# Last stage's attention of a fused decoder layer: the exponentials become the matmul's weights, values with a column of ones move, and the stage's written-out order is replaced

## The reference, cut to what matters

```python
nx = _rmsnorm(X, g1)                       # X: 8 x 512 x 256
Q = (nx @ Wq.T).reshape(B, S, 4, 64).transpose(0, 2, 1, 3)
Kc = nx @ Wkc.T                            # one K and one V of width 64 for all 4 heads
Vc = nx @ Wvc.T
attn = softmax(einsum('bhsd,btd->bhst', Q, Kc) / 8, axis=-1)
out = einsum('bhst,btd->bhsd', attn, Vc)
X = X + out.transpose(0, 2, 1, 3).reshape(B, S, d) @ Wo.T
# then: norm, router (top 2 of 8 experts), shared expert, experts
```

## Time and profile before

| | |
|---|---|
| median of 3 executions | 1976.12 us (1971.84 to 1981.54) |
| profiled execution | 1981.15 us, span 1979.4 us |
| granted TensorE clock, mean | 0.959 |
| TensorE / VectorE / ScalarE / GpSimd busy over the span | 90% / 71% / 60% / 55% |
| `moe_attention` | about 1342 to 1750 us of the span |
| one turn in it | 45.4 us (mean of five: 1438.3 to 1665.5 us) |

### The profile page before, as it was taken

How to read it: one execution, slowest core, us unless ns; L and a number is a source line. 1 busy time by engine, 2 the same in 40 slices (tenths; PEclk the granted TensorE clock), 3 DMA queues, 4 the chain that set the end, 5 groups by cost and what they waited for, 6 DMA issues and landing times. The chain is left out here.

```text
span 1979.4 us, 46476 instructions
## 1 busy us (share of the span) xinstructions
PE 1779.3 (90%) x16808; PEld 986.1 (50%) x16808; DVE 1415.2 (71%) x3433; ACT 1185.8 (60%) x2285; POOL 1096.3 (55%) x1102
## 2 busy tenths in 40 slices
PE   5899999999999999889999999986998999779994
PEld 2566767676766767633233333222333344346662
DVE  5766676667676766477777888766699987757677
ACT  2666566566666666367677787782566666435552
POOL 2766666666676666543243433123667776646664
PEclk9999999999999999989899999897999999889998
DMA  6422222223222232321333212301001110224465
GB/s 197 103 66 66 66 66 66 66 66 76 66 66 66 60 82 66 71 65 34 54 65 65 50 37 46 60 11 38 22 23 44 49 49 33 73 73 130 116 209 201
DMA packets 102545, 141.36 MB, mean 71 GB/s; under 512 B 16400, under 2 KB 66352, under 8 KB 102320
## 3 DMA queue, kind: packets, MB, share of 16 engines
q1 hardware_dynamic: 95408, 119.44, 25.6%
q0 software_dynamic: 6912, 18.95, 2.7%
HBM read 53.77 MB, written 33.90 MB: 44 GB/s over the span
## 5 line engine op out<-in xcount | busy, mean ns | idle before, releaser
L821 POOL TENSOR_TENSOR a_P_lo<-a_PR,a_P_hi 128x384 f16<-128x384 f32 (+1 forms) x384 | 378.9, 1001 | 269.7 <-ACT a_PR L630 126.8
L1387 DVE TENSOR_REDUCE x_NM<-x_pm 128x1 f32<-128x512 f32 x512 | 342.5, 688 | 104.0 <-PE x_pm L1123 101.6
L1308 ACT ACTIVATE x_PR<-x_pS 128x512 f32<-128x512 f32 x512 | 300.8, 601 | 118.4 <-PE x_pS L1139 112.5
L739 DVE CUSTOM_DVE_ANT_0 a_pm<-a_pm,a_causal 128x128 f32<-128x128 f32 (+3 forms) x512 | 243.4, 511 | 133.2 <-PE a_pm L511 129.6
L630 ACT ACTIVATE a_PR<-a_pS 128x384 f32<-128x384 f32 (+1 forms) x384 | 202.4, 527 | 148.5 <-PE a_pS L535 145.6
L633 ACT ACTIVATE a_P_hi<-a_pS 128x384 f16<-128x384 f32 (+1 forms) x384 | 203.6, 530 | 26.6 <-PE a_pa L554 26.6
L1151 PE MATMUL x_pa<-x_PR,x_V 128*32 128x256 f32 x2048 | 170.9, 408 | 1.6
L511 PE MATMUL a_pm<-a_KA,a_QA 128*128 128x128 f16 (+3 forms) x512 | 125.3, 305 | 39.4 <-issue 21.6
L533 PE MATMUL a_pS<-a_QA,a_KA 128*128 128x512 f16 (+3 forms) x512 | 153.6, 303 | 1.2 <-ACT a_P_hi L633 0.8
L1462 POOL TENSOR_TENSOR x_res<-x_res,x_OT 128x256 f32<-128x256 f32 x32 | 23.5, 734 | 232.0 <-DVE x_OT L1396 232.0
L534 PE MATMUL a_pS<-a_QB,a_KB 128*128 128x512 f16 (+3 forms) x512 | 148.9, 304 | 0.0
(11 more groups left out here) (410 smaller groups left out, 5065.6 us busy)
## 6 DMA issues: line engine op xcount, KB each, us to landing
a_QA<-a_nat_q_hi SPq DMA_DIRECT2D x128, 128.0 KB, 2.3
first_keys<-sent SPq DMA_DIRECT2D x80, 129.0 KB
a_KA<-a_nat_k_hi SPq DMA_DIRECT2D x64, 128.0 KB, 2.3
a_KA<-a_nat_k_lo SPq DMA_DIRECT2D x64, 128.0 KB, 2.4
a_QB<-a_nat_q_lo SPq DMA_DIRECT2D x64, 128.0 KB, 2.3
a_KB<-a_nat_k_hi SPq DMA_DIRECT2D x64, 128.0 KB, 2.3
e_ga<-back SPq DMA_DIRECT2D x16, 512.0 KB
first_keys<-in_w SPq DMA_DIRECT2D x12, 512.0 KB
```

The source lines that it names most:

```text
L739: eng.tensor_tensor_reduce(out=pm[i % 2][:, 0:n], in0=pm[i % 2][:, 0:n], in1=causal[:, T - n:T], scale=1.0, scalar=NEG, op0=ALU.add, op1=A ...
L821: eng.tensor_tensor(P16[1][:, m % RH, 0:n], PR[:, m % RF, 0:n], P16[0][:, m % RH, 0:n], ALU.subtract).then_inc(s_el, 1)
L1308: eng.activation(PR[:, kc, j, :], pS[i % 2][:, :], ACT.Exp, scale=SCALE).then_inc(s_e, 1)
L1387: eng.tensor_reduce(NM[:, v % 2, c:c + 1], ring_bank("max", v, n)[:, :], AX.X, ALU.max, negate=True).then_inc(s_red, 1)
```

## The change

V gets a 65th column of ones, so that the sum of the exponentials comes out of the same matmul as the weighted values. In `weighted_values` the roles are exchanged: a block of 128 keys x 128 queries of PR is the weight matrix and the 65 columns of V move; the result has queries on partitions, 4 blocks of 65 columns in a bank, side 0 in pv and side 1 in pu. VectorE then takes 4 reciprocals (128 x 4) and 4 multiplications (128 x 256) per sequence, directly from the banks. Since the result is not transposed any more, Y is split in hi and lo (Y16, by ScalarE and GpSimd), TensorE transposes both (YT, 2 x 8 transposes) into pv and pu, and ScalarE copies these out (2 x 1024 float16 columns). Gone: the four additions on GpSimd, the four PU steps, Ln and Exp of the reciprocal, the copy PC. The table of positions is replaced as a whole by LAST_PLACE, for all engines.

```diff
-    V = sb("V", [P, 2, TT, D], F32)
-    ones32 = sb("ones32", [P, D], F32)
+    V = sb("V", [P, 2, TT, D + 1], F32)
 ...
             eng.wait_ge(s_e, 16 * b + 2 * i + 2)
             if i == 0:
                 eng.wait_ge(s_vo, b + 1)
-                after(eng, s_x1, 2 * b - 1)
+                after(eng, s_x1, 2 * b)
             elif i == TT:
-                eng.wait_ge(s_pc, b + 1)
+                eng.wait_ge(s_y, 4 * b + 2)
             for side in range(2):
-                m = eng.matmul(pv[half(side), :], V[:, par, kc, :], PR[:, i % 4, side, :], start=(kc == 0), stop=(kc == TT - 1))
+                for t in range(TT):
+                    m = eng.matmul(value_bank(side)[:, t * OW:t * OW + D + 1], PR[:, i % 4, side, t * P:(t + 1) * P], V[:, par, kc, :],
+                                   start=(kc == 0 and t == 0), stop=(kc == TT - 1), skip_group_check=True)
             m.then_inc(s_av, 1)

-        def exp_sums(b, j):
-            eng.wait_ge(s_ad, 4 * b + j + 1)
...
-            for side in range(2):
-                m = eng.matmul(pu[half(side), :], ones32[:, :], PR[:, 2 * j % 4, side, :], start=(j % 2 == 0), stop=(j % 2 == 1))
-            m.then_inc(s_pu, 1)
+        def turn_values(b, z):
+            eng.wait_ge((s_yh, s_yl)[z], 2 * b + 2)
+            if z == 0:
+                eng.wait_ge(s_y, 4 * b + 4)
+            for pair in range(2):
+                for t in range(TT):
+                    o = pair * T + t * P
+                    m = eng.transpose(value_bank(z)[:, :].bitcast(F16)[:, o:o + P], Y16[z][:, t, pair, :], k.id16[:, :])
+            m.then_inc(s_yt, 1)
...
                 for side in range(2):
                     eng.wait_ge(s_s, 16 * b + 2 * i + side + 1)
-                    after(eng, s_pu, 4 * b + i // 2 - 1)
+                    after(eng, s_av, 8 * b + i - 3)
                     eng.activation(PR[:, i % 4, side, :], pS[side][:, :], ACT.Exp, scale=SCALE).then_inc(s_e, 1)
...
-                eng.activation(RS[:, :], pu[:, :], ACT.Ln).then_inc(s_ln, 1)
-                eng.wait_ge(s_ln, 2 * b + pair + 1)
-                eng.activation(RS[:, :], RS[:, :], ACT.Exp, scale=-1.0).then_inc(s_rc, 1)
...
+                eng.activation(YT[z][:, :, :].rearrange("p a t -> p (a t)"), value_bank(z)[:, :].bitcast(F16), ACT.Copy).then_inc(s_yo, 1)
...
+                eng.reciprocal(RC[:, i, :], o[:, :, D]).then_inc(s_rc, 1)
+                eng.wait_ge(s_rc, 4 * b + i + 1)
+                eng.tensor_tensor(Y[:, :, pair, side, :], o[:, :, 0:D], RC[:, i, :].unsqueeze(2).to_broadcast([P, TT, D]),
+                                  ALU.mult).then_inc(s_y, 1)
...
-                eng.tensor_tensor(both, both, PR[:, (2 * j + 1) % 4, :, :], ALU.add).then_inc(s_ad, 1)
...
+LAST_PLACE = {
...
+    ("PE", "QK"): (7.224, 7.224, 8.938),
+    ("PE", "V"): (10.868,),
+    ("PE", "MX"): (1.193, 12.227, 16.689, 16.689, 28.543, 38.17, 41.193, 44.517),
+    ("PE", "NM"): (47.989,),
+    ("PE", "S"): (50.126, 55.366, 60.956, 71.226, 78.982, 83.035, 84.579, 89.259),
+    ("PE", "AV"): (81.063, 82.196, 82.196, 83.139, 87.157, 87.157, 91.495, 95.421),
+    ("PE", "YT"): (96.968, 96.968),
+    ("PE", "WO"): (100.505, 103.017),
...
+    ("PE", "O"): (153.929, 166.983),
+    ("PE", "RK"): (168.09,),
...
+    ("DVE", "QK"): (9.055, 9.055, 26.038),
+    ("DVE", "MX"): (26.038, 34.297, 34.297, 34.297, 34.297, 44.068, 44.068, 44.068),
+    ("DVE", "O"): (173.183, 173.183),
+    ("DVE", "R1"): (149.546,),
+    ("DVE", "R2"): (155.441,),
...
```

More of the change, by code:

```diff
@@ L1895, in moe_block @@
         moe_experts(nc, keep, inner, k, x_res, out_dram, B, groups, shared)
+LAST_TURN = 46.0
+LAST_PLACE = {
+    ("PE", "XT"): (3.925, 3.925),
+    ("PE", "QK"): (7.224, 7.224, 8.938),
[6 more added lines that the diff above has]
+    ("PE", "WO"): (100.505, 103.017),
+    ("PE", "FT"): (129.781, 129.781),
+    ("PE", "RT"): (140.121,),
+    ("PE", "H1"): (140.121, 142.004),
+    ("PE", "H3"): (142.004, 144.691),
+    ("PE", "O"): (153.929, 166.983),
+    ("PE", "RK"): (168.09,),
+    ("ACT", "N4"): (-8.58,),
+    ("ACT", "QK"): (3.454, 3.454, 10.717),
+    ("ACT", "V"): (10.717,),
+    ("ACT", "NM"): (37.914,),
+    ("ACT", "S"): (50.382, 60.419, 60.419, 66.48, 82.489, 82.489, 82.489, 82.489),
+    ("ACT", "YT"): (93.194, 93.194),
+    ("ACT", "YS"): (87.017, 88.012),
+    ("ACT", "F1"): (109.87,),
+    ("ACT", "F3"): (124.532,),
+    ("ACT", "H1"): (133.787, 133.787),
+    ("ACT", "H3"): (149.031, 149.031),
+    ("ACT", "R1"): (135.636,),
+    ("ACT", "R3"): (164.025,),
+    ("ACT", "SPLIT"): (44.585, 48.725),
+    ("DVE", "N1"): (-40.185,),
+    ("DVE", "N4"): (3.18,),
+    ("DVE", "XT"): (4.955, 4.955),
+    ("DVE", "QK"): (9.055, 9.055, 26.038),
+    ("DVE", "MX"): (26.038, 34.297, 34.297, 34.297, 34.297, 44.068, 44.068, 44.068),
+    ("DVE", "NORM"): (86.986, 86.986, 95.768, 95.768),
+    ("DVE", "WO"): (121.77, 121.77),
+    ("DVE", "F3"): (130.533,),
+    ("DVE", "FT"): (134.203, 134.203),
+    ("DVE", "RT"): (141.504,),
+    ("DVE", "H1"): (141.504, 143.365),
+    ("DVE", "H3"): (143.365, 146.171),
+    ("DVE", "O"): (173.183, 173.183),
+    ("DVE", "R1"): (149.546,),
+    ("DVE", "R2"): (155.441,),
+    ("DVE", "R3"): (176.043,),
+    ("DVE", "RK"): (172.773,),
+    ("DVE", "SPLIT"): (86.6, 86.6),
+    ("POOL", "NP1"): (7.955,),
+    ("POOL", "NP2"): (7.955,),
+    ("POOL", "YS"): (121.764, 121.764),
+    ("POOL", "NP3"): (144.717,),
+    ("POOL", "XR"): (144.717,),
+    ("POOL", "H3"): (171.595, 171.595),
+    ("POOL", "SC"): (207.713, 207.713, 207.713, 207.713),
+    ("SP", "MR"): (66.11,),
+}
@@ L2026, in at @@
         if step == "TB":
-            return b * TURN + PLACE["DVE", "RK"][0] + 0.1 + GAP * i
+            return b * LAST_TURN + LAST_PLACE["DVE", "RK"][0] + 0.1 + GAP * i
         if step in ("TL", "LD"):
-            return (groups[1].first - 1) * TURN + PLACE["DVE", "RK"][0] + GAP * Tables.STEPS + (0.01 if step == "TL" else 1.0)
-        return b * TURN + PLACE[engine, step][i]
+            return (groups[1].first - 1) * LAST_TURN + LAST_PLACE["DVE", "RK"][0] + GAP * Tables.STEPS + (0.01 if step == "TL" else 1.0)
+        return b * LAST_TURN + LAST_PLACE[engine, step][i]
     def at_split(engine, n):
@@ L2146, in sums @@
         def sums(b):
-            for j in range(4):
-                yield at("PE", "PU", b, j)
-                exp_sums(b, j)
+            for z in range(2):
+                yield at("PE", "YT", b, z)
+                turn_values(b, z)
             for h in range(2):
                 yield at("PE", "WO", b, h)
-                eng.wait_ge(s_y, 2 * b + 2)
-                eng.wait_ge(s_yl, 2 * b + 2)
+                eng.wait_ge(s_yo, 2 * b + 2)
                 for tt in range(2):
@@ L2310, in splits @@
                 weights.high(eng, n)
-        side_by_side(over(back), over(route), over(sums), over(values), over(exponentials), over(front), over(norm, 1), splits())
+        side_by_side(over(back), over(route), over(sums), over(exponentials), over(front), over(norm, 1), splits())
     def vector_program(eng):
@@ L2342, in sums @@
         def sums(b):
[L2343 to L2352, removed]
+            for i in range(H):
+                pair, side = i // 2, i % 2
+                yield at("DVE", "NORM", b, i)
+                o = value_bank(side)[:, 0:TT * OW].rearrange("p (t e) -> p t e", e=OW)
+                eng.wait_ge(s_av, 8 * b + TT * (pair + 1))
+                after(eng, s_yl, 2 * (b - 1) + pair + 1)
+                eng.reciprocal(RC[:, i, :], o[:, :, D]).then_inc(s_rc, 1)
+                eng.wait_ge(s_rc, 4 * b + i + 1)
+                eng.tensor_tensor(Y[:, :, pair, side, :], o[:, :, 0:D], RC[:, i, :].unsqueeze(2).to_broadcast([P, TT, D]),
+                                  ALU.mult).then_inc(s_y, 1)
             for h in range(2):
@@ L2583, in gpsimd_program @@
         eng.sem_inc(s_pre, 1)
-        side_by_side(over(back), over(route), over(sums), over(adds), over(norm, 1))
+        side_by_side(over(back), over(route), over(sums), over(norm, 1))
     def sync_program(eng):
```

66 lines of the change are left out of this document (21 added, 45 removed), and 6 rows, old and new, of the table PLACE.

## The result

The changed kernel takes 2028.1 us in the median (2021.7 to 2030.7, four executions) against 1975.9 us (1971.8 to 1981.5) in the same measurement: a ratio of 1.026, interval 1.022 to 1.029. The forecast was slower, by 1.3%, 2002 us; it became slower by 2.6%, twice as much, and within the range. The profiled execution took 2029.5 us, its span 2027.7.

The account below looks back on a forecast made before the run. TensorE's issue was taken as the bound, with about 3 us per turn lost behind VectorE. Terms +20 - 16 + 27 - 5 = +26 us gave 2002 us against the median of 1976.1, 1.3% slower; range 1955 to 2032.

Parts of the forecast that it names:

- The price of a value matmul: TensorE's AV steps: 128 records per sequence at 0.107 us each, set by the weight load; 14.0 us in all.
- the changes of shape: TensorE switching between full array and halves: 0.1 us each, 19 left of 34 per turn, 1.5 us less.
- Quick load: Rival, AV: weights load at the transposes' rate, 0.056 us a record, AV 7.5 us, total 1956 us; chance 0.16.
- load and stream one after the other: Rival, AV: load and stream don't overlap, 0.162 us a record, 56 us more, 2058 us; chance 0.06.
- YT: New transposes of Y on TensorE: 0.9 us per sequence, their inputs' delay covered by some 5 us of other work.
- The removed wait: TensorE's wait at XT for the low half of the normalized rows goes: -16 us.
- The added waits: TensorE waits at MX, RK and behind QK in the new order: 3.8 us per turn, seven times, +27 us.
- The other engines: VectorE even, GpSimd rid of four 2.45 us additions, ScalarE lighter; priced only through TensorE's waits.
- A turn of 48 to 49 us: Sign in the profile after: each turn of the stage takes 48 to 49 us, against 45.4 before.
- the last rival, the clock: More standing still lowers TensorE's clock more often; a stretch costs at most half its length; no chance given.

Follow-up runs that it names:

- mx_halves: Changed kernel with MX3 and MX4 moved apart, R1 and R2 later, and each value block as two 64-column halves; 1975.5 us, ratio 1.005.
- sc_later: Changed kernel with GpSimd's scatter issued later, behind its low rows of Y; 2017.9 us, ratio 1.027.
- cols33: Changed kernel with only 33 of the 65 value columns moving in each value matmul; 2064.3 us, ratio 1.051.
- col_halves: Changed kernel with each block of 128 weights as two of 64, side by side in TensorE's column halves; 1973.7 us, ratio 1.003.
- mx_only: Changed kernel with MX3 behind S3, MX4 behind O1 and VectorE's O0 ahead of MX3's reductions; 1981.0 us, ratio 1.006.
- sc_later_again: The changed kernel with the later scatter, same program run once more, on chip 3 instead of 13; 2031.6 us, ratio 1.028.
- old_order: Changed attention in the order of steps of the kernel before, with YT, NORM and YS placed in by hand; 2027.8 us, ratio 1.029.

## Why the prediction was right, and where its size was off

The direction and the price on which it hung came as forecast. The size did not: +52 us between the medians where the forecast had +26, and inside the range only because its upper side was kept wide. The two profiled executions are 48.3 us apart, of which 42.2 lie in the seven turns, 7.7 behind the last NM and -1.6 ahead of the first.

- **The price of a value matmul** (all hung on it): forecast 0.107 us a record, set by the load and not by the stream. Found: four matmuls, eight records, every 0.89 us, 0.112 each; with half the columns the same. A load record is 192 ns long by itself, as the slope of the earlier trace rows gives it (136 and 54), so at 0.112 apart each overlaps the next. Right, 0.005 low: AV 14.7 us a turn against 14.0. AV and YT together cost 3.9 us more than AV and PU did, where the forecast had 2.5 with the changes of shape. Quick load and "load and stream one after the other" are both out; 65 columns of streaming are hidden wholly.
- **YT** at 0.9 us, and covered: 0.90, with 0.6 us of waiting in all turns. Right, as long as GpSimd's scatter ends before; `mx_halves` shows the price without this cover, 6 us a turn.
- **The removed wait**, -16 us: XT and FT fell from 4.91 to 1.88 where no signal is held, 3.0 a turn. The wait itself is gone in the changed kernel as well, but there "issue" gaps fill its place (5.19).
- **The added waits**, 3.8 a turn: too high. Where no signal is held, MX rose by 1.0 (forecast 2.3), RK and O by 0.5 (0.7), QK and V by 0.2 (0.8), S by 1.0 (none): 2.7.
- **The other engines** got lighter as worked out (multiplications of 0.42 us); TensorE stayed the fullest, and no run shows what the relief was worth.
- **A turn of 48 to 49 us**: 48.4 in the profile of `sc_later`, 52.7 in that of the changed kernel. The span of `sc_later` is 26.7 us above that of before, forecast +26, but that is luck: +20.7 in the turns, +12 in the end, which holds the price of the later scatter, and -6 ahead of the first turn. And against before on its own chip its median is 48.5 us higher.
- **The step that was off in size** is the last rival, the clock, which I let only "widen the upper side", with no term for TensorE standing still while all is ready. In the changed kernel's profile this fills four of the seven turns (against `sc_later` H +2.3 and XT +3.3 a turn, S -0.7), with 6.8 us a turn at half clock, where `sc_later` has none. No term stood for the end either (+7.7). The trace of before showed held signals as well, up to 4.1 us late; I had not looked.

An estimate of the changed kernel where no signal is held: the start and the turns of `sc_later` (1362.3 and 318.2 us) and the end of `cols33` (314.9), both of chip 13, give 1997 us with the 1.75 around the span, and 2005 to 2010 with the 8 to 13 us by which the other executions of `sc_later` exceed its profiled one. Against 1969.4 on that chip this is 1.4 to 2.1% slower. It was not measured.

What is shown: a value matmul costs its load (`cols33`), and with the load split in two the changed attention is within 0.6% of before (`col_halves`); with MX3 and MX4 moved it is within 0.9% even at the full price of the load (`mx_only`). So the 2.6% have more than one part, and these don't add up: both together (`mx_halves`, 1.005) win no more than each alone. What was only argued: that all executions of the changed kernel have held signals; their times (2021.7 to 2030.7) fit it, one profile shows it. How much of the 52 us the held signals are is not shown: before had them too, and `sc_later` loses 2.7% on the chip where its profile has none. What stays open: why signals are held, and what the chip or the hour has to do with it. The scatter is under way each time, but it is so too in the profiles of chip 13, and the sizes and times of the instruction fetches do not sort the cases.

## What to carry to other kernels

Before the exponentials are made the weights and the narrow matrix moves, compare the load with the stream: 128 float32 columns of weights cost 0.112 us for 65 columns of use, while the kernel before used its load of 64 for 512 columns; as two column halves the same work took 0.47 us a side instead of 0.89. When a new order comes with a change, look in the old trace for late signals and for "issue" gaps too, not only for waits on data: two steps one behind the other on the same buffer (MX3 behind MX2) cost about 1 us a turn. One profile is one execution: where its time is at the edge of the others, take another before reading it. And before two variants are compared by their traces, see that they ran on the same chip: here a behaviour that seemed to follow the order of steps followed the chip or the hour.

## What the runs showed of the hardware

- Matmuls on 128 columns of float32 weights begin 0.112 us apart at full clock and 0.213 at half, with 65 as with 33 columns moving. With 33 (`cols33`) the granted clock was 0.92 over the whole span, against 0.95 in the changed kernel and 0.96 in `sc_later` on the same chip.
- The Trainium skill ("TensorE: Matmul & The Clock Gate", LDWEIGHTS) gives P/1.2 ns, 107 for 128 columns; the trace agrees within 5% at full clock.
- While a scatter of eight indirect transfers was running, TensorE's signals reached other engines up to 9 us late in all four profiles of chip 3 (26 to 39 such signals in a stage), and at most one was late in each of the eight of chip 13. In the held turns TensorE stood still for up to 1.8 us at a time with nothing to wait for (the changed kernel), and the clock went to half behind such gaps, for 17 us in the longest case (`sc_later_again`, from 1562.8 us).
- The clock also fell to half without any held signal: behind waits (`old_order`, 5.7 us a turn) and in `cols33`, where TensorE had no "issue" gap in the stage (22.6 us a turn).
